# Sixteen-headed cross-attentions: where the values copy and the transposes back stand in two queues

## The reference

```
qh, kh, vh = heads(q @ Wq + bq), heads(ctx @ Wk + bk), heads(ctx @ Wv + bv)
att = softmax(qh . kh / sqrt(8), over the keys)      # L1: with a mask over the keys
out = att @ vh, heads side by side again
x = x + (out @ Wo + bo)
```

## Time and profile before

| | |
|---|---|
| time, median of 3 runs | 1788.22 us (1783.66 to 1791.61) |
| profiled execution | 1790.74 us, its span 1789.0 us |
| PE | 1257.9 us busy (70% of the span) |
| PEld | 834.9 us (47%) |
| DVE | 1175.0 us (66%) |
| ACT | 768.9 us (43%) |
| POOL | 155.2 us (9%) |
| softmax part on DVE, 96 units | L1916 116.8 us, L1920 117.5 us |
| exponentials on ACT, 96 units | 101.7 us |
| transposes of probabilities on PE, 768 | 107.0 us |
| TensorE's granted clock, mean of the span | 0.818 of full speed |

### The profile page before, as it was taken

How to read it: one execution, slowest core, us unless ns; L and a number is a source line. 1 busy time by engine, 2 the same in 40 slices (tenths; PEclk the granted TensorE clock), 3 DMA queues, 4 the chain that set the end, 5 groups by cost and what they waited for, 6 DMA issues and landing times.

```text
span 1789.0 us, 25090 instructions
## 1 busy us (share of the span) xinstructions
PE 1257.9 (70%) x8858; PEld 834.9 (47%) x8870; DVE 1175.0 (66%) x2883; ACT 768.9 (43%) x1410; POOL 155.2 (9%) x132
## 2 busy tenths in 40 slices
PE   5998889954799999799933798987889700001665
PEld 2555555533478878745522454554554400001444
DVE  2654557877556676487767576885764389994446
ACT  1544346754355445346645433664434314430221
POOL 2210103100000000012011001110000000000001
PEclk7888789987899999889966776999999955555678
DMA  3000300000000000000000000000002300001000
GB/s 116 13 13 13 138 7 7 7 1 0 1 1 1 1 1 7 7 7 7 7 1 0 1 1 7 13 1 1 0 0 55 79 19 0 0 1 53 18 0 23
DMA packets 28805, 28.11 MB, mean 16 GB/s; under 512 B 12192, under 2 KB 23456, under 8 KB 27808
## 3 DMA queue, kind: packets, MB, share of 16 engines
q1 hardware_dynamic: 28704, 26.76, 4.9%
HBM read 20.20 MB, written 6.55 MB: 15 GB/s over the span
## 4 chain that ended last, share of the span: by engine, by line
PE 46%; issue 21%; DVE 21%; ACT 8%; DVEq 2%; POOL 2%; DMA 1%; SPq 1%; POOLq 0%; ACTq 0%
PE PSA L842 3%; PE PSA L995 3%; PE PSA L832 3%; PE PSA L1280 2%; PE PSA L682 2%; DVE BIG L2474 2%; PE PSA L688 2%; PE PSA L665 2%; PE PSA L1012 2%; PE PSA L975 2%; PE PSA L949 2%; ACT BIG L1483 2%; PE PSA L961 2%; PE PSA L956 2%; DVE BIG L2466 2%
## 5 line engine op out<-in xcount | busy, mean ns | idle before, releaser
L1307 PE MATMUL PSA<-W,TMP 128*128 128x128 f32 x32 | 8.3, 441 | 215.2 <-DVE TMP L2496 215.2
L1490 ACT ACTIVATE QK<-PSA 128x512 f32<-128x512 f32 x192 | 104.7, 595 | 110.3 <-PE PSA L842 110.3
L528 POOL TENSOR_TENSOR RSTD<-VEPS,HALF 128x4 f32<-128x4 f32 x50 | 50.7, 1015 | 947.3 <-DVE VEPS L1801 947.3
L1920 DVE TENSOR_TENSOR BIG<-PSA,MX 128x1024 f32<-128x1024 f32 x96 | 117.5, 1224 | 12.3 <-PE PSA L842 9.3
L832 PE MATMUL PSA<-BIG 32*128 32x512 f32 x384 | 114.3, 685 | 15.0 <-DVE BIG L1920 13.9
L1916 DVE TENSOR_REDUCE MX<-PSA 128x8 f32<-128x1024 f32 x96 | 116.8, 1216 | 6.2 <-PE PSA L832 5.6
L1483 ACT ACTIVATE BIG<-BIG 128x1024 f32<-128x1024 f32 x96 | 101.7, 1059 | 25.2 <-DVE BIG L1920 25.2
L842 PE MATMUL PSA<-K,BIG 128*128 128x128 f32 x768 | 107.0, 285 | 6.4 <-ACT BIG L1483 4.8
L842 PEld LDWEIGHTS PSA<-K,BIG 128*128 128x128 f32 x768 | 90.8, 146 | 40.1 <-ACT BIG L1483 28.1
L1307 PEld LDWEIGHTS PSA<-W,TMP 128*128 128x128 f32 x32 | 7.1, 327 | 216.4 <-DVE TMP L2496 216.4
L534 POOL TENSOR_SCALAR BIG<-BIG,COLS 128x512 f32<-128x512 f32 x52 | 80.5, 1564 | 261.1 <-ACT BIG L1475 140.4
(11 more groups left out here) (373 smaller groups left out, 3059.7 us busy)
## 6 DMA issues: line engine op xcount, KB each, us to landing
CTX<-in_ctx_t SPq DMA_DIRECT2D x16, 256.0 KB, 3.1
W<-in_w SPq DMA_DIRECT2D x1, 2048.0 KB, 7.2
W<-in_w SPq DMA_DIRECT2D x1, 1412.0 KB, 11.8
ROWS<-in_rows SPq DMA_DIRECT2D x1, 1232.0 KB, 8.9
scratch_q<-TMP SPq DMA_DIRECT2D x4, 256.0 KB, 2.0
W<-scratch_q SPq DMA_DIRECT2D x64, 16.0 KB
W<-in_w SPq DMA_DIRECT2D x2, 512.0 KB, 10.7
scratch_q<-BIG SPq DMA_DIRECT2D x4, 256.0 KB, 2.3
```

Of the source, the lines that this page charges most:

```text
L528: pool.tensor_tensor(RSTD[:, 0, :], VEPS[:, 0, :], HALF[:], ALU.pow).then_inc(ln_rstd.sem, 1)
L1490: act.activation(PT[:, m % 2, c, :], PS[4 + c], ACT.Copy).then_inc(p_ready.sem, 1)
L1920: dve.tensor_tensor(tile(PH[:, m % 2, :], 8), s, last(high, P), ALU.subtract).then_inc(shifted.sem, 1)
```

## The change

On TensorE, `values_back(m // 2 - 1)` moves from ahead of `transposes(m + 1)` to behind `product(m)`, in the same even steps. On ScalarE, `exp(m + 1)` moves ahead of `values_out(m // 2 - 1)`. No instruction is added or removed, and no wait is changed; every other engine's list stays as it is. L0's self-attention has functions of the same names with the old order and is not touched.

```diff
--- before.py
+++ after.py
@@ -902,11 +902,11 @@
                     if e == 5 and more:
                         project_values(it + 1, misc())
                         freed = v_ready, v_ready.at(p, it + 1)
-                    if e % 2 == 0 and m:
-                        freed = values_back(m // 2 - 1)
                     if m + 1 < GROUPS * HALVES:
                         transposes(m + 1)
                     product(m)
+                    if e % 2 == 0 and m:
+                        freed = values_back(m // 2 - 1)
                     if e == 1 and it == 0:
                         next_xnt(0, misc())
                         freed = xnt_ready, xnt_ready.at(p, 0)
@@ -1514,10 +1514,10 @@
                     if m and e == 3 and more and p != "L1x":
                         queries(it + 1, PS[7])
                     copies(m)
+                    if m + 1 < GROUPS * HALVES:
+                        exp(m + 1)
                     if m and m % 2 == 0:
                         values_out(m // 2 - 1)
-                    if m + 1 < GROUPS * HALVES:
-                        exp(m + 1)
                     if m and e == 1 and it == 0:
                         xnt_next(p, 0)
                     if m and e == 1 and it and p != "L0x":
```

## The result

The changed kernel takes 1815.55 us (median of 4 runs, 1811.30 to 1816.65), the kernel before 1787.89 beside it (4 runs, 1783.66 to 1791.61). The ratio is 1.0151 with a 95% interval of 1.0123 to 1.0179: slower, as forecast, but by 27.7 us and not by 9.4. The profiled execution of after took 1816.53 us with a span of 1814.8.

The account below looks back on a forecast made before the run. No engine is full in L0x, so chains decide, chiefly VectorE's through the moved back-transposes. L0x +8.0, L1x +2.6, L2x -1.2 sum to +9.4: 1800.1 profiled, 1797.6 us as median, own range 1793 to 1803.

Parts of the forecast that it names:

- VectorE's loop: Subtract, exponential, transposes, product, back-transposes, reciprocal, next odd subtract: 6.42 us a pair of units, where a plain pair took 5.30.
- D: L0x's pair of units in which VectorE also makes the normalised rows: forecast 8.44 us, was 7.08.
- A: L0x's pair of units with VectorE's kept-test and update of X: forecast 9.02 us, was 7.91.
- B: L0x's pair of units decided by the loop of ScalarE and TensorE: forecast 7.05 us, was 7.33.
- C: L0x's pair of units in which VectorE also does the moments: forecast 7.91 us, 6.9 before.
- The reciprocal's wait: VectorE's wait for the back-transposes: grows from 44.3 to some 70 us, about 1.1 to 1.4 a pair in L0x.
- The end of L0x: Last transposes of L0x no longer wait for a bank copy: saves 0.9 us.
- L1x and L2x: The two later cross-attention stages: L1x +2.6 us over three groups, L2x -1.2 us.
- the rival that the clock falls: TensorE drops to 1.2 GHz; one group at the low clock adds 6 to 18 us: 1804 to 1816; chance 0.12.
- a sign of being wrong: Includes a clock under 1.00 between the 20th and the last 5 us of a stage.
- VectorE's lead: Rival: VectorE's lead returns each group and swallows the wait; L0x +2.4, sum +3.8, 1792 us; chance 0.18.
- ScalarE's loop: Rival: nothing of VectorE's waits and ScalarE's and TensorE's gains decide; about 11 us less, 1777; chance 0.08.

Follow-up runs that it names:

- warm: Changed kernel with useless identity products added on TensorE at two places of each L0x group, where it would pause; 1805.63 us, ratio 1.0071.
- pause2: Kernel before, all orders unchanged, with two useless 128x512 VectorE operations behind L0x's kept-test; 1800.22 us, ratio 1.0063.
- not_L0x: Kernel before with the change made in L1x and L2x only; 1791.32 us, ratio 1.0003.
- between_cover: Changed kernel with transposes back between next transposes and product, and VectorE's kept-test, moments and normalised rows ahead of normalising; 1778.69 us, ratio 0.9925.
- between: Changed kernel with the transposes back moved between the next unit's transposes and the product; 1782.38 us, ratio 0.9958.
- tensor_half: Changed kernel with the values copy put back ahead of the exponential, so only TensorE's edit remains; 1814.00 us, ratio 1.0115.

## Why the prediction was right in direction and wrong in size

**What bounds the kernel, and VectorE's loop: right.** In warm, with the clock at 1.00, D is 8.34, A 9.01, B 7.03, C 7.91 (forecast 8.44, 9.02, 7.05, 7.91), and L0x 95.07 for 95.1. That the sum fits so well is part luck: each D is 0.1 us under its forecast, and the second C, at 8.19, 0.28 over. The reciprocal's wait there is 70.0 us for some 70, 1.0 to 1.6 us a pair in L0x (76.9 in after, with the low clock), and the copies' waits left L863.

**The end of L0x: half right.** From the last exponential to L1121, 8.90 us (400.59 to 409.49) in place of 9.33: 0.43 saved, forecast 0.9.

**L1x and L2x: right, L1x a little too high.** L1x +1.5 for +2.6 (D 7.96 as forecast; A, B and C together 25.62 for 26.0), L2x -1.1 for -1.2. Without the clock the sum of the loops is 8.9+1.5-1.1=+9.3, where the forecast had 8.9+2.6-1.2=+10.3 for them. Its +9.4 took 0.9 off for the end of L0x; with the 0.43 measured there the sum is +8.9. The two misses, 1.0 in the loops and 0.5 at the end, partly cancel.

**The step that failed: the clock at 1.00.** The sum used lengths at 2.4 GHz throughout, and the rival that the clock falls had 0.12, with the argument that TensorE's work per pair is the same, spread over some 10% more time. The argument looked at the spread and not at the single pauses, and pauses are what pause2 shows to bring the low clock and warm to keep it away when filled. The low clock came between the 20th and the last 5 us of L0x, which the forecast itself had named as a sign of being wrong. Pair A grew by 1.1 us, and TensorE's stall for the XNT copy (1.34 us for its weight loads, 0.52 for its matmuls) was gone from it: both reappear in one place, ahead of the next scores, where 0.71 us became 2.14. D gained a pause of 1.9 to 2.2 ahead of L920 and the scores behind it, and the last group one of 3.05. Before, no pause in L0x's loop was over 0.78 until the last group (1.42). The length of the pause could have been worked out beforehand: in before, the same stretch from scores to scores (298.69 to 306.68, 7.99 us) less its stalls of 0.52 and 0.71 has 6.76 us of work, and A's forecast 9.02 less that is 2.26. That it would lower the clock could not be read there: before pauses 2.16 us behind L0x's last exponential, at 379.45, and the clock stays at 1.00 for the next 4 us. The rival's own time was 1804 to 1816, and the clock cost 7.3 to 10.4 us in the three profiles, inside its 6 to 18. So the rival was written down and given too little chance. That its price holds is partly luck: it was worked out for one whole group at the low clock, and what came were four shorter stretches. The Trainium skill (TensorE: Matmul & The Clock Gate, section "A second HAM failure mode: psum-queue depth-cycling") tells of a kernel in which TensorE idles for a moment between groups of matmuls so often that its clock swings between the two levels. The three profiles of after agree: pauses of 1.9 to 3.1 us, four low stretches in each.

**What was not explained by it.** Loops and clock give 16.6 to 19.7 us. The two later profiles of after, 1805.84 and 1806.86 us, lie 16.2 and 17.2 above the 1789.69 us that before takes in that comparison, and agree. The first pair of profiles differs by 25.8: 5.6 arose ahead of unit 7's exponential in L0x and 4.6 behind L2x's last one. Of the 5.6, 5.4 lie ahead of the stage's first exponential, where all 14 kernels are the same; their profiles put it at 261.07 to 267.13 us (before 261.56 and 264.01, after 266.61 to 267.13), so I don't put the 5.6 down to the change. Behind L2x's last exponential the code is the same but for the stage's last steps, and the 14 profiles take 568.7 to 577.7 us for it: 572 in both of before, 574.3 to 577.2 in the three of after, 572.6 in not_L0x, which has the change in L2x. No run tells whether the 4.6 belong to the change. So of the 18.3 us by which the first comparison missed the forecast, about 10 stay without a cause.

**The rivals.** VectorE's lead does not return: D and A of L0x take the forecast lengths in each group of warm. ScalarE's loop did not decide with this order, but for B, where the forecast had it; in between_cover, with transposes back and VectorE's other work both out of the wait, the pairs are shorter than before's, and the time is 12.3 us less (1790.96 in that comparison).

**Left open.** Why a pause of 2.14 us lowers the clock at one time and not at another. Why between is faster than before by more than its loops. Whether the low clock would vanish from between_cover too (it fell once there, behind 1.72 us) was not tried.

## What to carry to other kernels

When an instruction is moved off one engine's path, look at who waits for it, and close that loop step by step: here the chain of five hops gave the pairs that it decides to 0.1 us at a clock of 1.00, all but one. Then go through TensorE's new schedule for its pauses, not only for its mean share of busy time, and price the work behind each new pause at the low clock as well, as something that may come. Where a wait can't be removed, put the waiting engine's independent work in front of it: the same orders with VectorE's work ahead of the wait went from 1.5% slower (0.9% in the later runs) to level, and with the transposes back ahead of the product to 0.75% faster.

## What the runs showed of the hardware

I had not expected the granted clock to fall behind pauses this short. In the 14 profiles, from about 284 us to the end of L0x's loop, TensorE paused 30 times for 1.9 to 3.1 us, and within the next 4 us the clock was below 1.00 behind 20 of them; of 61 pauses of 0.7 to 1.9 us it fell behind 3. No bound between the two follows: it fell once behind 0.72 (with a second pause of 0.54), and stayed at 1.00 behind 2.49 in between. A low stretch cost its pair 0.8 to 5.2 us (12.21 in tensor_half for 7.03 in warm), as the wait of the reciprocal grew with it (2.56 us in B of after, 1.03 in warm). And a stage can get shorter by useless work in TensorE's pauses: L0x's loop takes 95.07 us in warm, with 48 more products, and 102.41 to 105.47 in after.
